# One block for both layers: recurrence tables begun at the last gate product, second-layer token transposes between the last down groups, recurrent buffers placed anew

## The reference

```
xn = layernorm(x)
s  = silu(xn @ w_gate.T);  the 688 entries of smallest |s| in each row of 1376 are set to 0
s  = (s * (xn @ w_up.T)) @ w_down.T
g  = silu(xn @ ternary(W).T + bias)
x  = x + s * g                                # first layer
xn = layernorm(x)
h  = xn @ Win.T + bin                         # width 64
for l in 0..3:                                # the recurrence
    y = silu(layernorm(h) * w + b)
    h = h + scl * Re(sum over earlier tokens of p**(distance) * y, plus a start term)   # p complex, per channel
    h = h + W2 @ silu(W1 @ layernorm(h) + b1) + b2
s  = layernorm(h) @ Wout.T + bout
g  = silu(xn @ (W + sum_e c_e B_e A_e).T + bias)
x  = x + s * g                                # second layer
```

## Time and profile before

| | |
|---|---|
| time, median of 3 runs | 631.98 us (630.73 to 631.99) |
| span of the profiled execution, first to last instruction | 629.6 us |
| its own time | not recorded beside the span; 2.3 us lie between the span and the runs' median |
| PE busy | 593.6 us (94% of the span) |
| DVE busy | 487.0 us (77%) |
| ACT busy | 339.8 us (54%) |
| POOL busy | 188.7 us (30%) |
| mean granted clock of TensorE | 0.974 of full speed |

### The profile page before, as it was taken

The page is one execution under the profiler, slowest core; times in us unless marked ns, Lnnn a source line. Parts: engine busy times, 40 slices in busy tenths (PEclk is TensorE's granted clock), DMA queues, the critical chain, the costliest instruction groups (busy, mean ns, idle before and its releaser), DMA issues. The chain is left out here.

```text
span 629.6 us, 8823 instructions
## 1 busy us (share of the span) xinstructions
PE 593.6 (94%) x2852; PEld 461.9 (73%) x2852; DVE 487.0 (77%) x940; ACT 339.8 (54%) x571; POOL 188.7 (30%) x303
## 2 busy tenths in 40 slices
PE   8969999999999999999999999999798999999775
PEld 6857888787888888888888888886575665656432
DVE  6998889888788789788878878768576676666556
ACT  6848567347428626744842862685463544455420
POOL 2332002001000200100100020079985666663344
PEclk9979999999999999999999999999979999999887
DMA  8801000020030020011003001091030000000015
GB/s 348 320 21 41 27 2 1 25 77 2 1 100 0 0 100 0 0 34 66 0 0 100 0 1 68 1 333 44 3 68 1 0 1 1 1 2 1 1 67 200
DMA packets 17194, 32.35 MB, mean 51 GB/s; under 512 B 3238, under 2 KB 3750, under 8 KB 17164
## 3 DMA queue, kind: packets, MB, share of 16 engines
q1 hardware_dynamic: 17164, 31.99, 14.6%
HBM read 24.63 MB, written 7.35 MB: 51 GB/s over the span
## 5 line engine op out<-in xcount | busy, mean ns | idle before, releaser
L857 DVE TENSOR_SCALAR_CACHE_REDUCE junk_d<-k_buf,cand 128x1376 int8<-128x1376 f32 x56 | 91.9, 1640 | 0.3
L650 ACT ACTIVATE junk_a<-k_buf,cand 128x1376 int8<-128x1376 f32 x56 | 80.5, 1437 | 0.6
L1197 PE MATMUL ps_a<-wd_hi,zt_hi 128*128 128x512 f32 (+1 forms) x176 | 71.9, 409 | 0.2 <-DVE zt_lo L976 0.2
L629 ACT ACTIVATE s_buf<-ps_a 128x1376 f32<-128x1376 f32 x16 | 21.1, 1318 | 94.0 <-PE ps_a L1164 89.4
L1197 PE MATMUL ps_a<-wd_hi,zt_lo 128*128 128x512 f32 (+1 forms) x176 | 69.2, 393 | 0.0
L1197 PE MATMUL ps_a<-wd_lo,zt_hi 128*128 128x512 f32 (+1 forms) x176 | 68.9, 391 | 0.0
L527 POOL TENSOR_TENSOR xres<-xres,gate 128x512 f32<-128x512 f32 x12 | 22.3, 1860 | 130.8 <-DVE gate L983 130.8
L519 POOL TENSOR_TENSOR rstd<-var_eps,expo 128x2 f32<-128x2 f32 x7 | 4.9, 703 | 164.9 <-DVE var_eps L779 164.9
L1164 PE MATMUL ps_b<-wu_hi,xt_hi 128*128 128x512 f32 (+1 forms) x192 | 52.4, 381 | 0.0
L1164 PE MATMUL ps_a<-wg_hi,xt_hi 128*128 128x512 f32 (+1 forms) x192 | 51.9, 379 | 0.0
L1164 PE MATMUL ps_a<-wg_lo,xt_hi 128*128 128x512 f32 (+1 forms) x192 | 50.8, 373 | 1.1 <-DVE wg_lo L762 1.1
(11 more groups left out here) (249 smaller groups left out, 1378.8 us busy)
## 6 DMA issues: line engine op xcount, KB each, us to landing
xres<-in_x SPq DMA_DIRECT2D x8, 512.0 KB, 3.3
out<-arena SPq DMA_DIRECT2D x16, 256.0 KB, 2.0
xin<-in_x SPq DMA_DIRECT2D x7, 512.0 KB, 3.9
x_scratch<-xres SPq DMA_DIRECT2D x6, 514.0 KB, 3.8
arena<-x_scratch SPq DMA_DIRECT2D x3, 1028.0 KB, 12.4
m_buf<-in_wg_t SPq DMA_DIRECT2D x2, 688.0 KB, 5.0
k_buf<-in_wg_t SPq DMA_DIRECT2D x2, 688.0 KB, 7.9
m_buf<-in_wu_t SPq DMA_DIRECT2D x2, 688.0 KB, 7.6
```

The lines of the kernel that those rows point to most:

```text
L629: act.activation(s_buf[:, t, :], ps_a[:].rearrange("p a n -> p (a n)")[:, 0:INNER], ACT.Silu).then_inc(s_ready, 1)
L650: act.activation(junk_a[:], k_buf[:, 1, :], ACT.Sign, bias=c, scale=-1.0, accum_out=below[:, 1:2]).then_inc(act_step, 1)
L857: dve.tensor_scalar(junk_d[:], k_buf[:, 0, :], c, -float(DROP), ALU.is_lt, ALU.add, accum_out=e).then_inc(cnt_dve, 1)
L1197: last = pe.matmul(ps_a[:, t, :], zs, ws[0:rows, c, :], start=(c == 0 and n == 0), stop=(c == CHUNKS - 1 and n == 2))
```

## The change

Both layers become one block: the barrier goes, and every place in memory that is reused is guarded by a semaphore.

- SP and POOL begin the second layer's loads and tables at `gate_done` of the last tile, one up product earlier. The loads of `x1` still wait for `up_done`.
- In `arena`, what POOL makes first and the fold now lie over the gate weights, `x1` behind them. The recurrence's small buffers move into `arena`; `xt` now lies over `wd_hi` and `wd_lo` in the order in which the tiles are taken, so that a tile can be taken when the down groups that read those weights are done (`covered_until`).
- POOL: the residual sums stand at other places among the doublings; the sixteenth of the coarse powers and the first 6 table products stand ahead of the last two residual sums.
- PE: 8 token tiles are transposed between the last three down groups; the other 8 lie as before around the first layer norm.
- DVE and ACT: the takes, the splits of the folded weights and the last `zt_low` are interleaved; DVE now takes tiles 8 to 11 too, ACT 4 fewer.

The core of the diff, with re-indented lines left out:

```diff
         def second_layer():
 
-                    sp.wait_ge(up_done, TILES)
+                sp.wait_ge(gate_done, TILES)
...
+                sp.wait_ge(up_done, TILES)
                 for i in range(3):
                     load_x1_group(sp, ORDER[i])
...
-                pool.wait_ge(up_done, TILES)
+            pool.wait_ge(gate_done, TILES)
...
-                residual(PAIRS - 1, 0, resident=True)
             tables_powers(pool, 0, 0, 2)
+            pool.wait_ge(up_done, TILES)
+            residual(PAIRS - 1, 0, resident=True)
+            tables_powers(pool, 0, 2, 4)
             residual(PAIRS - 1, 1, resident=True)
             norm2_root(pool, 1, 0, LOADED, expo[:])
-                tables_powers(pool, 0, 2, FINE_BITS)
-                tables_powers(pool, 1, 0, COARSE_BITS - 1)
+            tables_powers(pool, 0, 4, FINE_BITS)
+            pool.wait_ge(q_done, TILES)
+            pool.memset(row_f[:], 0.0).then_inc(rows_zero, 1)
+            tables_powers(pool, 1, 0, COARSE_BITS)
...
+            pool.wait_ge(mask_ready, TILES)
+            tables_some(0, 6)
             for t in range(2):
                 residual(PAIRS, t, resident=True)
+            norm2_root(pool, 2, LOADED, TILES, expo2[:, 0:TILES - LOADED])
+            second_root(0, 0)
...
+            def take_tile(i):
+                act.wait_ge(down_done, covered_until(i))
+                act.wait_ge(xt_ps, i + 1)
+                act.activation(xt[:, i, :], token_bank(i), ACT.Copy).then_inc(xt_a, 1)
...
+        LAST_DOWN = 2 * NG * PAIRS
+        def covered_until(i):
+            return LAST_DOWN - 2 if i < 4 else LAST_DOWN - 1 if i < 8 else LAST_DOWN
...
+            for i in range(2):
+                tokens(i)
+            down(last, 3)
+            zt_transpose(last, 5)
+            for i in range(2, 4):
+                tokens(i)
+            down(last, 4)
+            for i in range(4, 6):
+                tokens(i)
+            center_biases()
+            for i in range(6, PER_HALF):
+                tokens(i)
+            down(last, 5)
+            project_in(0)
             for i in range(PER_HALF, PER_HALF + 4):
                 tokens(i)
             variances(0, 0)
-                gates(4)
+            gates(6)
```

More of the change, by code:

```diff
@@ L148, in mixture_kernel @@
         u0 = over_weights(2, DEPTH)
+        rho = over_weights(DEPTH)
+        part = over_weights(2)
+        off = over_weights(KH + 2 * DEPTH)
+        bias_c = over_weights(DEPTH + 1)
+        carry = over_weights(2)
+        fold = over_weights(8, HID)
+        assert cursor[0] <= 2 * N_W
+        f_a, f_b, f_wt = fold[:, 0:2, :], fold[:, 2:4, :], fold[:, 4:8, :]
+        hs = [fold[:, 0:4, :], fold[:, 4:8, :]]
+        work = over_weights(4 * SEQ)
+        xn = work.rearrange("p (t n) -> p t n", n=HID)
+        w_re, w_im, u_re, u_im = (work[:, j * SEQ:(j + 1) * SEQ] for j in range(4))
+        sq = w_re
+        win = over_weights(KH, DIM)
+        stats2 = over_weights(2, 6)
+        rs2 = over_weights(TILES)
+        nmr = over_weights(TILES)
+        assert cursor[0] + TILES * ROW <= N_ARENA
+        x1 = over_weights(TILES, ROW)
         x1_in = [sem(f"x1_in{i}") for i in range(3)]
@@ L334, in mixture_kernel @@
             one = sb("one", [P, 1])
[L335 to L361, removed]
@@ new lines, in loads_before, with by_half @@
+        def loads_before(u):
+            return sum(slot_of(v) == slot_of(u) for v in range(u + 1))
+        def by_half(name):
+            return [sem(f"{name}{c}") for c in range(HALVES)]
+        last_in = sem("last_in")
+        rows_in = sem("rows_in")
+        rows_zero = sem("rows_zero")
+        rows_hi = sem("rows_hi")
+        rows_lo = sem("rows_lo")
+        xt_ps = sem("xt_ps")
+        xt_a = sem("xt_a")
+        xt_v = sem("xt_v")
+        xs_h = sem("xs_h")
+        xs_l = sem("xs_l")
@@ L1588, in _ @@
                     if feeds:
[L1589 removed]
+                        variance(n, d)
                     if l < DEPTH:
[L1591 to L1600 removed]
@@ L2075, in _program @@
+                else:
+                    pe.wait_ge(f_free, FF * DEPTH)
+                    output(4)
+                    output(5)
+                    variances(q, c)
+                    output(6)
+                    output(7)
+                    spread(q, c)
+                    pe.wait_ge(ln_o[c], q + 1)
+                    for m in range(PER_HALF, TILES):
+                        output(m)
 def _program(nc, args, out):
```

2915 lines of the change are left out of this document (1451 added, 1464 removed).

## The result

The median went from 631.68 us (6 runs, 630.73 to 632.21) to 629.13 us (6 runs, 626.75 to 630.83): ratio 0.9949, 95% interval 0.9926 to 0.9971. The kernel became faster by 0.5%, 2.5 us where 6.3 were forecast. The median lies 0.1 above the range; the ratio, taken on the 631.98 from which the forecast started, gives 628.8.

The account below looks back on a forecast made before the run. PE, busy 94%, was taken to set nearly all the time, with POOL's list deciding twice. Gains of 3.9 up to `h_in(0)` and 2.4 to `normed` gave 629.6 - 6.3 = 623.3, plus 2.3: 625.7 us, range 622.0 to 629.0.

Parts of the forecast that it names:

- Start of POOL's list: POOL's list begins at the last gate matmul's end, 397.99 instead of 406.46, 8.5 earlier; table start at 401.9.
- Length of the list: POOL's pieces up to the table products sum to 47.1, reaching 449.3 with 0.3 of wait; products end at 461.2.
- my added 2: Extra time put on POOL's six table products for disturbance by DVE, the middle of 0 to 3.7, above 9.85.
- Last sums: POOL's two residual sums behind the table products take 2.3, ending at 463.5; `h_in(0)` starts at 464.6, 3.9 won.
- From `h_in(0)` to `normed`: First layer norm: 5.6 instead of 8.0, 2.4 won, as POOL is free for the root; `normed` at 470.2.
- rival 3: PE's clock falls in new holes before `project_in(0)` and first `variances`, 3.3 of work lost, at worst 629.0; chance 0.07.
- 2 before the first `variances`: PE's hole ahead of the first `variances`, counted as about 2 within the 5.9 of holes allowed.
- Rival 2: POOL and DVE hold each other up more: gain only 1.3 to 4.8, typically 627.5 to 628.5; chance 0.2.
- my three signs of being wrong: Table products ending past 464, DVE's `token_stats` waiting for POOL over 3, or a clock of 0.5 behind two PE holes.
- PE behind `normed`: PE's work fits before the variance due at 480.6: without waits at 474.7, 5.9 of holes allowed.
- The 2.3 that I put between the span and the median: Whole kernel: 2.3 added to the forecast span of 623.3 to give the forecast median of 625.7.
- The hole at the barrier: PE idle 4.77 from 452.54, then 6.6 us at about half speed, some 3 us too many.

Follow-up runs that it names:

- f2_late: The changed kernel with SP's loads and POOL's list waiting for the last up product again (`up_done`), against the kernel before: 636.58 us, ratio 1.0073.
- e1_again: The changed kernel itself run once more, nothing altered, against the kernel before: 628.57 us, ratio 0.9929.
- g3_again: The changed kernel itself run again in a later group, nothing altered, against the kernel before: 628.79 us, ratio 0.9944.
- f3_sums: The changed kernel with POOL's last two residual sums ahead of the six table products, against the kernel before: 631.42 us, ratio 0.9998.
- e2_fill: The changed kernel with 24 identity transposes on PE filling the hole ahead of `variances(0, 0)`, against the kernel before: 627.13 us, ratio 0.9913.
- f1_both: The changed kernel with `h_in(0)` ahead of DVE's statistics and PE's gate steps spread over its waits, against the kernel before: 626.17 us, ratio 0.991.
- e3_hin: The changed kernel with `h_in(0)` ahead of the statistics of tiles 14 and 15 on DVE, against the kernel before: 625.95 us, ratio 0.9889.
- f4_before_fill: The kernel before with 40 identity transposes on PE behind its last down group, against the kernel before: 631.89 us, ratio 1.0003.
- e4_gates: The changed kernel with six gate steps ahead of `variances(0, 0)` on PE, against the kernel before: 626.92 us, ratio 0.9908.
- g2_takes_hin: The changed kernel with DVE's takes of tiles 5 and 7, `down_gate` and `h_in(0)` moved ahead of `rows_low`, against the kernel before: 628.23 us, ratio 0.9944.
- g4_order: The changed kernel with DVE's list cleared for `h_in(0)` and the first layer norm moved ahead on DVE, POOL and PE: 629.97 us, ratio 0.9955.

## Why the prediction was off by half

**Start of POOL's list: right.** It starts at T, and the table start stands at T + 4.0 (predicted 3.9). f2_late, slower than before without it, shows that the change depends on it.

**Length of the list: right in the sum, by two errors.** The products end at T + 63.2, as predicted (461.2 - 397.99). But they start at T + 53.5, not 51.3: the fold's data are waited for after all, 2.65 us (2.95 in e1_again, 1.32 in g3_again, whose products start at T + 52.7), and DVE's statistics held the root of 12 tiles for 1.62 instead of 0.3; the table start alone, 5.65 us for my 7.1, gave back 1.4. That the end came out right is luck. And the products took 9.7, as before, where I had put 2 on them. f3_sums shows 7.7 undisturbed, so the conflict costs POOL some 2 us in either order, and my added 2 wasn't on its list. It was on DVE's: two splits and two `rows_low` took 7.1 there (3.07, 2.12, 1.91), where 1.28 for two splits (450.60) and 1.22 for each `rows_low` (f3_sums) make 3.7. I had priced the conflict on one engine only. DVE still ended `down_gate(8, 1)` 0.4 ahead of POOL's products, so this didn't reach `h_in(0)`; the takes that stand behind those splits and the first `rows_low` are what PE waits 1.83 for. The SBUF page of the Trainium skill, section "SBUF: two separate sides", has a DVE instruction with two SBUF inputs and a GpSimd one exclude each other; a last product of 1.26 alone (f3_sums, 469.73) against 2.04 beside `rows_low`, `down_gate` and the first `xs_lo` split (460.05) agrees in direction, but the 3.7 that I worked out for it strictly didn't come on POOL.

**Last sums: mis-sized by 0.9.** 2.3 was their time beside an idle DVE; beside the `xs_lo` splits (2.73 for two) they took 3.2, in all three executions of the changed kernel. With this `h_in(0)` came at T + 67.4, 67.5 and 66.7 in three executions, for 66.6 predicted. Of the 3.9 forecast, 3.0 to 3.9 were won.

**From `h_in(0)` to `normed`: right for an undisturbed clock, and the clock was the failed step.** 5.6 was predicted; e1_again and e2_fill have 5.9. The profiled execution has 8.8 and g3_again 9.1, with the same instructions in the same order, since PE behind the 3.07 hole ran at PEclk 0.50. My rival 3 named this and gave it 0.07, because "the recurrence that follows is full of such waits". The trace of the kernel before says otherwise. From 490 to 590 PE never waits more than 0.23. Where it waits longer, near the end, the half clock is there too:

```profile
594.01 1.12 PE L1958 MATMUL ps_a<-ident,arena 128*128 128x128 f32 x4 [1.61 <-DVE arena L1713]
...
613.54 1.11 PE L1958 MATMUL ps_b<-ident,arena 128*128 128x128 f32 x4 [2.89 <-DVE arena L1713]
```

```profile
594.00:602.00 8.00, 5.24 (x18) 2.90 (x18) 1.71 (x3) 2.53 (x4) 1.10 (x1) 0.50 0.00 0
```

PEclk is 0.50 from 594 to 602, behind the 1.61 and through waits of 1.12 and 1.63, and 0.59 from 612 to 620, about the 2.89. So holes between 1.16 and 4.77 were there to be read, and they spoke for rival 3. Besides, I had counted "2 before the first `variances`" where the trace of the changed kernel has 3.07. The hole follows from my own numbers: `project_in(0)` done at 459.7, 2 of wait ahead of it and four token tiles of 0.43 give 463.4 for PE; `h_in(0)` at 464.6, with 0.75 for itself and 0.6 for the squares, gives 466.0 for its operand: 2.6 of hole. I had summed holes for their length and not compared these two times, which would have made rival 3 a main case. Its price was near: 3.3 of work lost, and the fall cost 2.9. That its 629.0 is almost the median of 629.13 is partly luck, since 1.6 of other losses (0.8, 0.3 and 0.5, below) are in the measured time of that execution and the median mixes executions. Rival 2, the mutual hold-up of POOL and DVE, gave a time near that too (627.5 to 628.5), but only 0.9 of the loss is of its kind. Of my three signs of being wrong, two didn't show (the products end at 462.09, `token_stats` waits 0.38); the clock of 0.50 behind a hole did.

**PE behind `normed`: "it fits" was 0.5 too good.** From `normed` to the variance of the other half it took 10.3 before and 10.8 to 10.9 in the changed kernel, with the half clock ahead of it and without. In the kernel before, PE waits 1.16 ahead of that variance; in the changed kernel it doesn't wait there, so its own work sets the time. f1_both, which has nine gate steps behind `project_in(1)` where the changed kernel has thirteen and moves four ahead of `variances(0, 0)`, waits 0.89 there and needs 10.3 again (T + 72.94 to T + 83.27). So it is the filling steps that stood in the way, though with `normed` 0.3 later than in e3_hin the variance of f1_both comes only 0.1 earlier.

**Summed up.** In the profiled execution: 6.3, less 0.8 at `h_in(0)`, 2.9 for the clock, 0.3 for the rest of that step (5.9 for 5.6) and 0.5 for PE, is 1.8, what is seen at the variance of the other half. In one without that fall, e1_again, it is 4.7 (T + 84.2 against 88.9), and 13 of the 18 executions belong to the slower group. The 2.3 that I put between the span and the median is 1.8 within one execution (630.83 and 629.0), which is small beside this. Where the half clock stands differs between executions of one program, so one trace of it tells a case, not the time.

**The hole at the barrier** was the first thing I read, and the least of it. f4_before_fill shows that of the half clock behind it at most 1.0 was on the path to `normed`. Since the sum was built on POOL's list, which counts from the table products, this cost the forecast nothing.

## What to carry to other kernels

After a change of order, work out the length of each remaining hole on PE from both sides (when it runs dry, and when the next operand comes), and treat one of 1 to 3 us, and not only of 5, as a half clock that may follow (here behind 3.07, 2.61, 1.82, 1.61 and once 1.15, though others of 1.2 to 1.9 passed at full clock); look in the trace of before for holes of that size and the clock behind them, in every part of the kernel; moving a piece of independent work into it (e4_gates), or bringing the operand forward (e3_hin), gives that time back. When one operand is pulled forward, look in every engine's list at what stands ahead of the next link: `h_in(0)` came 5 us earlier in g2_takes_hin and g4_order and `normed` at most 2.6. When two engines hold each other up, price it in both lists. The lowest median found is that of the changed kernel with `h_in(0)` ahead of the statistics, 625.95 us, 0.9889 of before.

## What was not expected of the hardware

- The same program has its stretch of PEclk 0.50 at different places in different executions: behind a hole of 3.07 and 3.06 in two, and in `project_in(0)` behind one of only 1.82 in a third (windows 460 to 464: PEclk 0.63), where two others held 1.00 through the same hole. e4_gates and e2_fill held it through 1.68 and 1.83; f2_late lost it behind 2.61, and f4_before_fill behind 1.15, which the kernel before passed at 1.00 with 1.16. What ties the fall to one or the other isn't settled.
- With 24 transposes that compute nothing the median is 1.4 us lower (628.57 to 627.13, on the same chip), and six runs lie within 626.96 to 627.65 in place of 626.87 to 629.0. The intervals of the two kernels overlap.
- Two residual sums back to back took 3.21 to 3.77 us beside DVE's splits, where two single ones earlier in the same list took 1.29 and 1.10.
- DVE pays for the same meeting: a row product of 1.22 alone took 1.91 and 2.12 beside POOL's table products, and two splits of 1.28 took 3.07.
